# One to four rounds of a threshold search in an iteration of the experts' loop, instead of three in each

## The chip, the cores and the metric

The kernel runs on one core of one Trainium2 chip. Its engines work side by side from their own instruction queues: TensorE (PE, with its weight loads as PEld), VectorE (DVE), ScalarE (ACT), GpSimd (POOL) and SyncE (SP, which here only issues loads). The metric is the device time of one launch in microseconds.

## What is computed

A small language-model tower: an n-gram embedding, an attention block of three branches, and a mixture of 32 experts in which each expert chooses the 256 tokens of 8192 that have the highest probability for it. The change lies in the last part:

```python
k = min(int(bs * C_CAP) // E, bs)             # 8192 // 32 = 256
h = xf @ W_router + b_router
Sm = jax.nn.softmax(h, axis=-1)
G_ek, idx_ek = jax.lax.top_k(Sm.T, k)
tokens = xf[idx_ek]
tok_g = tokens.reshape(NUM_GROUPS, GROUP_SIZE, k, H)
up = jnp.einsum('gjkh,ghf->gjkf', tok_g, W_up) + b_up[:, None, None, :]
act = jax.nn.silu(up).reshape(E, k, D_FF)
Eout = jnp.einsum('ekf,efh->ekh', act, W_down) + b_down[:, None, :]
weighted = G_ek[..., None] * Eout
y = jnp.zeros((bs, H)).at[idx_ek.reshape(-1)].add(weighted.reshape(-1, H))
```

## The kernel before

Embedding, attention and router take the first 950 us of the span. The function `experts` does the rest. It finds for each expert the probability of its 256th token, one bit of the float in a round, over 30 rounds (`BITS`), with a trial value per expert in `cand`. There are two searches, each for 16 experts. The first (h = 0) runs alone ahead of the loop. The second (h = 1) is spread over the first iterations of the loop over the experts, `ROUNDS = 3` rounds in each of the iterations e = 0 to 9; its result is first needed at the end of iteration 9 (`find_over(3)`), for the experts from number 16 on.

A round k is a chain through three engines. VectorE and ScalarE count what lies below the trial value (`count_bit`, L1699 and L1862), TensorE adds the counts over the partitions (`total`, L1491, L1493, L1495), and VectorE settles the bit (`settle_bit`, L1704, L1705, L1708), which writes the next trial value. The last round counts all on VectorE and is added with L1506 and L1507; then the thresholds are turned (L1512).

All engines run programs written out in order by hand. Iteration e of TensorE is `down(e)` (the second product of expert e, L1629), a round's total, `up(e + 1)` (the first product of the next expert, L1614), a round's total, `turn(e + 2)` (transposes of the tokens of the one after, L1599), `unread` (4 products that nobody reads, L1500), and a round's total. These are places 0, 1 and 3 in the new code's count. In iterations 0, 3 and 6 three more experts are ranked (`TRIPLE_AT`): `rank` comes ahead of `up`, `rows_before` (L1579) behind it, and `rows` (L1588) with 8 unread products behind `turn`. Iterations 1 and 10 also place a group of experts (`IN_LOOP`).

VectorE weighs the result of an expert (`weigh`, L1819, into yw) and copies the turned tokens (`copy_x`, L1812); in a ranking iteration it also makes `reached` (L1777) and the slots (`find_rows`, L1787 to L1799). GpSimd issues for each expert two gathers of tokens, four experts ahead (L1968, into xg), and two adding scatters of results (L1977, into out_h); the scatters of expert e wait for yw of e and for the scatters of e - 1 to land. With each gather of a new triple it also waits for the slots of that triple.

Of the kernel before, what the change touches and what calls it, by code (L numbers as in the profile page):

```python
# [43 lines left out]
BITS = 30  # L44
# [1230 lines left out]
def experts(nc, ctx, consts, con, prob, probT, bits, stored, scores, turned, mixed, table, w_up, b_up, w_down, out):  # L1275
# [11 lines left out]
    def sem(name):  # L1287
        return ctx.enter_context(nc.semaphore(name))
# [72 lines left out]
    cand_ok = [sem(f"cand_ok{h}") for h in range(SHARES)]  # L1361
# [34 lines left out]
    def lap(e, buffers):  # L1396

        return (e // buffers + 1) * 16
# [8 lines left out]
    PLACE_BANK = (2, 3, 0, 1, 0)  # L1407
    IN_LOOP = {1: 2, 10: 3, 13: 4}

    ROUNDS = 3  # L1410
    UNREAD_TO = 14

    def rounds_of(e):

        return range(min(e * ROUNDS, BITS), min((e + 1) * ROUNDS, BITS))

    def total_at(h):

# [58 lines left out]
    def _(pe):  # L1477
# [8 lines left out]
        def total(h, k):  # L1486

            pe.wait_ge(cand_ok[h], k + 1)
            if h > 0:
                pe.wait_ge(counted[h], k + 1)  # L1490
            pe.matmul(total_at(h), fours[:], limits[:, 0:1], start=True, stop=False)  # L1491
            pe.wait_ge(counted_a[h], k + 1)
            pe.matmul(total_at(h), less_one[:], count_a[:, h:h + 1], start=False, stop=False)  # L1493
            pe.wait_ge(counted[h], k + 1)
            pe.matmul(total_at(h), less_two[:], count[:, h:h + 1], start=False, stop=True).then_inc(totalled[h], 1)  # L1495
# [19 lines left out]
        def totals(ks):  # L1515
            for k in ks:
                if k < BITS - 1:
                    total(1, k)
                else:
                    total_last(1)  # L1520
                    thresholds(1)
# [70 lines left out]
        def turn(e):  # L1592
            pe.wait_ge(x_in[e % XB], HALVES * lap(e, XB))
            if e >= 2:
                pe.wait_ge(xt_v, e - 1)
            if e - 3 in IN_LOOP:
                pe.wait_ge(chosen_ok, IN_LOOP[e - 3] + 1)
            for half in range(HALVES):
                last = pe.transpose(scores[:, (e % 2) * 512 + half * P:(e % 2) * 512 + (half + 1) * P],  # L1599
                                    xg[:, e % XB, half, 0:C], ident)  # L1600
            last.then_inc(xt_t, 1)
# [55 lines left out]
        turn(1)  # L1657
        for e in range(NE):
            down(e)
            totals(rounds_of(e)[0:1])  # L1660
            if e in TRIPLE_AT:
                rank(TRIPLE_AT[e])
            if e + 1 < NE:
                up(e + 1)
            if e in TRIPLE_AT:
                rows_before(TRIPLE_AT[e])
            totals(rounds_of(e)[1:2])
            if e + 2 < NE:
                turn(e + 2)
            if e in IN_LOOP:  # L1670
                sums(IN_LOOP[e])
            if e in TRIPLE_AT:
                if rounds_of(e):
                    pe.wait_ge(cand_ok[1], rounds_of(e)[1] + 2)
                rows(TRIPLE_AT[e])
            if e in IN_LOOP:
                places_within(IN_LOOP[e])
                places_before(IN_LOOP[e])
            elif e < UNREAD_TO:
                unread(8 if e in TRIPLE_AT else 4, (e + 1) % 2)  # L1680
            totals(rounds_of(e)[2:])

    @block.vector
    def _(dve):
# [30 lines left out]
        def later_count(ks):  # L1715
            for k in ks:
                count_bit(1, k, SPLIT if k < BITS - 1 else HC)

        def later_settle(ks):
            for k in ks:  # L1720
                settle_bit(1, k)
                if k == BITS - 1:
                    keep_thresholds(1)
# [21 lines left out]
        def find_over(g):  # L1745
            compare(over, g, ALU.is_gt).then_inc(over_ok, 1)
# [82 lines left out]
        dve.tensor_scalar(odd[:, 1, :].bitcast(I32), probT[:, HC + SPLIT:2 * HC].bitcast(I32), 1, None, ALU.bitwise_or  # L1829
                          ).then_inc(odd_later, 1)  # L1830
        for e in range(NE):
            first, second, third = (rounds_of(e)[j:j + 1] for j in range(ROUNDS))
            later_count(first)
            weigh(e)
            later_settle(first)
            later_count(second)
            if e in TRIPLE_AT:
                reach(TRIPLE_AT[e])
            later_settle(second)
            if e + 2 < NE:  # L1840
                copy_x(e + 2)
            if e in TRIPLE_AT:
                find_rows(TRIPLE_AT[e])
            later_count(third)
            if e in IN_LOOP:
                choose(IN_LOOP[e])
            later_settle(third)
            if e > 0 and e + 1 in IN_LOOP:
                find_over(IN_LOOP[e + 1])
                find_ties(IN_LOOP[e + 1])  # L1850

    @block.scalar
    def _(act):
        act.activation(less_one[:], K("same"), ACT.Identity, scale=-4.0).then_inc(less_ok, 1)
        act.activation(less_two[:], K("same"), ACT.Identity, scale=-8.0).then_inc(less_ok, 1)
        act.wait_ge(odd_ok, 2)
        act.activation(probT.rearrange("p (h c) -> p h c", h=SHARES)[:, :, (CT - 1) * P:],
                       scores[:, 0:SHARES * P].rearrange("p (h c) -> p h c", h=SHARES), ACT.Identity).then_inc(prob_copied, 1)

        def count_bit(h, k):  # L1860
            act.wait_ge(cand_ok[h], k + 1)
            act.activation(below_a[:], odd[:, h, :], ACT.Sign, bias=cand[:, h:h + 1].bitcast(F32), scale=-1.0,  # L1862
                           accum_out=count_a[:, h:h + 1]).then_inc(counted_a[h], 1)

        def later_count(ks):
            for k in ks:
                if k < BITS - 1:
                    count_bit(1, k)

        with act.Fori(0, BITS - 1) as k:  # L1870
            count_bit(0, k)

        act.wait_ge(bup_in, 16)
        act.activation(warm[:], bup[:, 0:1], ACT.Silu)
        act.wait_ge(far_in, 16)
        act.wait_ge(made_g, 1)

        def keep_sums(g):
            act.wait_ge(sums_t, g + 1)
            at = slice(pairs(g)[0], pairs(g)[-1] + 1)  # L1880
            act.activation(tile_sums[:, :, at], down_bank[:, 0:2 * NE // PAIR].rearrange("t (m j) -> t m j", m=2)[:, :, at],
                           ACT.Identity).then_inc(sums_a, 1)

        def keep_ranks(g):
            e0, e1 = TRIPLES[g][0], TRIPLES[g][-1] + 1
            act.wait_ge(rank_t, g + 1)
            act.activation(ranks[:, e0:e1, 0:P], rank_bank[0:TT, 0:(e1 - e0) * P].rearrange("p (e t) -> p e t", t=P),
                           ACT.Identity).then_inc(rank_a, 1)

        def find_rows(g):  # L1890
            e0, e1, m = TRIPLES[g][0], TRIPLES[g][-1] + 1, len(TRIPLES[g])
            act.wait_ge(row_t, HALVES * g + 2)
            for i, e in enumerate(TRIPLES[g]):
                k = e * HALVES + 1
                act.activation(less[:, k, :], row_bank(1)[:, i * RW:i * RW + P], ACT.Sign,  # L1895
                               bias=K("slotmid")[:, 1:2], scale=-1.0, accum_out=n_less[:, k:k + 1])
            at = slice(e0 * HALVES + 1, (e1 - 1) * HALVES + 2, HALVES)
            act.activation(tile_no[:, at], row_bank(1)[:, 0:m * RW].rearrange("p (i r) -> p i r", r=RW)[:, :, P],
                           ACT.Identity).then_inc(row_a, 1)

        def silu(e):
            act.wait_ge(up_t, e + 1)
            if e >= 2:
                act.wait_ge(down_t, e - 1)
            for c in range(FC):
                n = FP if c < FC - 1 else FP - 1
                k = e // GROUP * FC + c
                last = act.activation(hid[0:n, e % 2, c, :], up_bank[0:n, c * TOPK:(c + 1) * TOPK], ACT.Silu,  # L1908
                                      bias=bup[0:n, k:k + 1])
            last.then_inc(hid_a, 1)  # L1910

        keep_sums(0)
        keep_ranks(0)
        find_rows(0)
        keep_ranks(1)
        keep_sums(1)
        find_rows(1)
        keep_ranks(2)
        find_rows(2)
        act.wait_ge(ones_set, 2)  # L1920
        silu(0)
        act.wait_ge(odd_later, 1)
        for e in range(NE):
            later_count(rounds_of(e)[0:1])
            if e in TRIPLE_AT:
                keep_ranks(TRIPLE_AT[e])
            later_count(rounds_of(e)[1:2])
            if e + 1 < NE:
                silu(e + 1)
            if e in IN_LOOP:  # L1930
                keep_sums(IN_LOOP[e])
            if e in TRIPLE_AT:
                find_rows(TRIPLE_AT[e])
            later_count(rounds_of(e)[2:])

    @block.gpsimd
    def _(pool):
# [103 lines left out]
```

## Time and profile before

| | us |
|---|---|
| median of 3 runs | 1228.16 (1227.95 to 1229.41) |
| profiled execution, its own time | 1231.34 |
| its span, first to last instruction | 1229.6 |
| start of the experts' part (first search) in the span | 950.6 |
| first `down` of the loop | 1013.91 |
| last scatter ends | 1227.4 |

All readings of the timeline are microseconds from the start of the span. "Iteration e" is the stretch from TensorE's `down(e)` to its `down(e + 1)`. "PEclk" and "granted clock" are TensorE's, as a share of 2.4 GHz; it has the two levels 1.00 and 0.50 (1.2 GHz), and a value between them is a mean over a stretch.

### The profile page before, as it was taken

Reading aid. Unit: us, or ns where it says so; the run is one execution under the profiler, and the core shown is the slowest. Engines: PE = TensorE matmul, PEld = TensorE weight load, DVE = VectorE, ACT = ScalarE, POOL = GpSimd, SP = SyncE. Lnnn points to the kernel's source line nnn. Section 1 sums busy time; section 2 is a strip of 40 time slices with the busy share of each in tenths; the row PEclk is TensorE's granted clock in tenths of the full one; section 3 lists DMA queues with packets and bytes.
Section 4 is the critical chain, followed back from the end, with each engine's and each line's share of the span. In section 5 each row is a group of like instructions: output and inputs, shape, how many; then the busy total and the mean of one; then the engine's idle time right before and its main releaser. Section 6 shows DMA issues by size and latency. Waiting matters only on the chain. (4 is left out here: it accounts for less than half of the span.)

```text
span 1229.6 us, 23394 instructions
## 1 busy us (share of the span) xinstructions
PE 1065.2 (87%) x7550; PEld 944.5 (77%) x7550; DVE 830.4 (68%) x2686; ACT 677.6 (55%) x1742; POOL 736.0 (60%) x1200
## 2 busy tenths in 40 slices
PE   5689999999999999999999999999995357788672
PEld 4569888988988898998899899888884135666551
DVE  5346777787877778777777877787676777664220
ACT  0346756756676676666576666666663545434220
POOL 6356676677467547746864775353445027678885
PEclk9989999999999999999999999999997558889876
DMA  3011011010001001010100101000001103344442
GB/s 106 18 33 27 14 29 33 14 36 21 24 25 35 25 10 39 25 30 25 35 26 10 35 25 34 12 10 12 14 16 40 41 18 70 68 81 86 85 71 29
DMA packets 49085, 42.64 MB, mean 35 GB/s; under 512 B 6728, under 2 KB 44488, under 8 KB 48840
## 3 DMA queue, kind: packets, MB, share of 16 engines
q0 software_dynamic: 18432, 22.04, 9.5%
q1 hardware_dynamic: 30536, 19.13, 5.1%
q8 instruction: 62, 1.02, 0.3%
q14 instruction: 55, 0.45, 0.1%
HBM read 27.51 MB, written 13.63 MB: 33 GB/s over the span
## 5 line engine op out<-in xcount | busy, mean ns | idle before, releaser
L657 PE MATMUL mixed<-v,pT 128*128 128x131 f32 x2560 | 318.7, 276 | 3.6 <-DVE o L920 3.2
L657 PEld LDWEIGHTS mixed<-v,pT 128*128 128x128 f32 x2560 | 301.5, 190 | 5.0 <-issue 4.5
L913 DVE TENSOR_REDUCE neg_max<-scores 128x1 f32<-128x1024 f32 (+1 forms) x192 | 198.8, 1035 | 48.9 <-PE scores L444 48.8
L1150 POOL DMA_INDIRECT gram<-in_emb,ids x192 | 189.9, 989 | 64.9 <-issue 52.4
L1078 ACT ACTIVATE probs<-scores,neg_max 128x1024 f32<-128x1024 f32 (+1 forms) x192 | 186.2, 970 | 38.8 <-DVE neg_max L913 38.3
L1087 ACT ACTIVATE pT<-turned 128x512 f32<-128x512 f32 x219 | 130.0, 593 | 74.8 <-PE turned L638 73.9
L1201 POOL TENSOR_TENSOR zb<-row,gate 128x384 f32<-128x384 f32 x64 | 54.5, 851 | 144.2 <-DVE gate L948 143.8
L638 PE MATMUL turned<-con,probs 128*128 128x128 f32 x876 | 126.7, 275 | 7.6 <-ACT probs L1078 3.5
L1977 POOL DMA_INDIRECT out_h<-yw,slots x64 | 102.4, 1601 | 36.1 <-issue 20.6
L638 PEld LDWEIGHTS turned<-con,probs 128*128 128x128 f32 x876 | 101.6, 141 | 22.3 <-ACT probs L1078 8.9
L1968 POOL DMA_INDIRECT xg<-token_table,slots x64 | 64.5, 1008 | 67.6 <-DVE slots L1799 49.0
L919 DVE BATCH_NORM_STATS2 st<-mixed 128x6 f32<-128x128 f32 x192 | 56.1, 292 | 59.3 <-PE mixed L657 57.7
L442 PE MATMUL scores<-k_hi,xT_hi 128*128 128x512 f32 x192 | 82.2, 428 | 0.3 <-DVE k_lo L818 0.3
L956 DVE SCALAR_TENSOR_TENSOR u<-o,gate_r,u 128x128 f32<-128x128 f32 x128 | 78.2, 611 | 4.5
L1087 ACT ACTIVATE pT<-mixed 128x512 f32<-128x512 f32 x101 | 60.0, 594 | 30.5 <-PE mixed L638 30.0
L1908 ACT ACTIVATE hid<-scores,bup 114x256 f32<-114x256 f32 (+1 forms) x96 | 38.4, 471 | 69.3 <-PE scores L1614 69.2
L443 PE MATMUL scores<-k_lo,xT_hi 128*128 128x512 f32 x192 | 75.8, 395 | 0.0
L444 PE MATMUL scores<-k_hi,xT_lo 128*128 128x512 f32 x192 | 75.8, 395 | 0.0
L1629 PE MATMUL mixed<-wd,hid 114*128 114x128 f32 x384 | 61.4, 321 | 9.4 <-issue 9.4
L1218 POOL TENSOR_SCALAR shift<-mv 128x1 f32<-128x1 f32 x64 | 14.6, 229 | 89.4 <-DVE mv L967 87.4
L1205 POOL TENSOR_TENSOR zb<-zb 128x128 f32<-128x128 f32 x128 | 60.6, 474 | 10.0
L1629 PEld LDWEIGHTS mixed<-wd,hid 114*128 114x128 f32 x384 | 55.7, 228 | 12.5 <-issue 12.0
(350 smaller groups left out, 2550.2 us busy)
## 6 DMA issues: line engine op xcount, KB each, us to landing
wd<-in_w_down SPq DMA_DIRECT2D x32, 171.0 KB
token_table<-w SPq DMA_DIRECT2D x16, 320.0 KB, 2.4
out_h<-h SPq DMA_DIRECT2D x16, 256.0 KB, 2.3
gram<-in_emb,ids POOLq DMA_INDIRECT x192, 2.5
wu<-in_w_up SPq DMA_DIRECT2D x8, 170.5 KB, 4.0
w<-in_weights SPq DMA_DIRECT2D x1, 1174.0 KB, 6.4
xg<-token_table,slots POOLq DMA_INDIRECT x64, 3.1
out_h<-yw,slots POOLq DMA_INDIRECT x64
```

Source lines behind the costliest of these rows:

```text
L442: pe.matmul(dst, lhs[0], rhs[0], start=first_one, stop=False)
L443: pe.matmul(dst, lhs[0], rhs[1], start=False, stop=False)
L444: return pe.matmul(dst, lhs[1], rhs[0], start=False, stop=last_one)
L638: last = pe.transpose(dst[:, j * P:(j + 1) * P], probs[:, n % 2, half * 512 + j * P:half * 512 + (j + 1) * P], ident)
L657: last = pe.matmul(mixed[:, 0:C + 3], pT[:, n % 2, j * P:(j + 1) * P], vals[:, 0:C + 3], start=(j == 0), stop=(last_half and j == half * 4 ...
L913: dve.tensor_reduce(neg_max[:, n % 4:n % 4 + 1], scores[:, (n % 2) * S:(n % 2) * S + width], AX_X, ALU.max, negate=True).then_inc(maxed, 1)
L956: last = dve.scalar_tensor_tensor(out=u[:, m, br, :], in0=o[:, n % 4, br, 0:C], scalar=gate_r[:, m, br:br + 1], in1=u[:, m, br - 1, :] if ...
L1078: act.activation(probs[:, n % 2, 0:width], scores[:, (n % 2) * S:(n % 2) * S + width], ACT.Exp, bias=neg_max[:, n % 4:n % 4 + 1], accum_ou ...
L1087: act.activation(pT[:, n % 2, half * 512:half * 512 + 512], shared_bank(TURNED_ON[n, half]), ACT.Identity).then_inc(pT_ok, 1)
L1150: pool.indirect_dma_start(gram[:, t % 4, g, :], None, emb[g], bass.IndirectOffsetOnAxis(ap=ids[:, s, t, g:g + 1], axis=0)).then_inc(gather ...
L1629: last = pe.matmul(down_bank[:, half * C:(half + 1) * C], hid[:, e % 2, c, half * P:(half + 1) * P], wd[:, e % EB, c, :], start=(c == 0), ...
L1977: pool.indirect_dma_start(rows_out, bass.IndirectOffsetOnAxis(ap=slots[:, k:k + 1], axis=0), yw[:, e % EB, half, :], None, compute_op=ALU. ...
```

## The change

The number of rounds in an iteration now comes from a table. The iterations 0 to 9 hold 1, 3, 4, 1, 4, 4, 2, 4, 4 and 3 rounds, where each held 3. The sum is 30 in both. There is a new place 2, directly behind `turn` on TensorE and behind `copy_x` on VectorE. One round sits at place 1; two sit at 1 and 3; three at 0, 1 and 3, as before; four at all places. Everything else keeps its order.

```diff
-    ROUNDS = 3
+    ROUND_AT = (0, 1, 4, 8, 9, 13, 17, 19, 23, 27, BITS)
+    PLACES = 4
     def rounds_of(e):
-        return range(min(e * ROUNDS, BITS), min((e + 1) * ROUNDS, BITS))
+        return range(ROUND_AT[e], ROUND_AT[e + 1]) if e + 1 < len(ROUND_AT) else range(0)
+    def rounds_in(e, place):
+        in_order = ((), (1,), (1, 3), (0, 1, 3), (0, 1, 2, 3))[len(rounds_of(e))]
+        return [k for k, at in zip(rounds_of(e), in_order) if at == place]
...
             down(e)
-            totals(rounds_of(e)[0:1])
+            totals(rounds_in(e, 0))
...
-            totals(rounds_of(e)[1:2])
+            totals(rounds_in(e, 1))
             if e + 2 < NE:
                 turn(e + 2)
+            totals(rounds_in(e, 2))
             if e in IN_LOOP:
                 sums(IN_LOOP[e])
             if e in TRIPLE_AT:
-                if rounds_of(e):
-                    pe.wait_ge(cand_ok[1], rounds_of(e)[1] + 2)
+                for k in rounds_in(e, 1):
+                    pe.wait_ge(cand_ok[1], k + 2)
                 rows(TRIPLE_AT[e])
...
-            totals(rounds_of(e)[2:])
+            totals(rounds_in(e, 3))
...
             later_count(third)
+            later_settle(third)
+            later_count(fourth)
             if e in IN_LOOP:
                 choose(IN_LOOP[e])
-            later_settle(third)
+            later_settle(fourth)
```

ScalarE's list changes in the same way (its counts at places 2 and 3 both stand behind `find_rows`).

TensorE, iteration 4, from the total behind `up(5)` to `down(5)`, before (turned<-... are the three products of a total, scores<-con,xg is `turn`, scores<-slot_bf is `unread`, mixed<-wd,hid is `down`):

```order
L1491 MATMUL turned<-limits,fours 128x1
L1493 MATMUL turned<-count_a,less_one 128x1
L1495 MATMUL turned<-count,less_two 128x1
L1599 MATMUL scores<-con,xg 128x128 x2
L1500 MATMUL scores<-slot_bf,ones_bf 128x256 x4
L1491 MATMUL turned<-limits,fours 128x1
L1493 MATMUL turned<-count_a,less_one 128x1
L1495 MATMUL turned<-count,less_two 128x1
L1629 MATMUL mixed<-wd,hid 128x128 x6
```

and now:

```order
L1497 MATMUL turned<-limits,fours 128x1
L1499 MATMUL turned<-count_a,less_one 128x1
L1501 MATMUL turned<-count,less_two 128x1
L1605 MATMUL scores<-con,xg 128x128 x2
L1497 MATMUL turned<-limits,fours 128x1
L1499 MATMUL turned<-count_a,less_one 128x1
L1501 MATMUL turned<-count,less_two 128x1
L1506 MATMUL scores<-slot_bf,ones_bf 128x256 x4
L1497 MATMUL turned<-limits,fours 128x1
L1499 MATMUL turned<-count_a,less_one 128x1
L1501 MATMUL turned<-count,less_two 128x1
L1635 MATMUL mixed<-wd,hid 128x128 x6
```

A third total stands between `turn` and the unread products, which move behind it.

TensorE, the end of iteration 3 and the begin of iteration 4, before (turned<-ranks,reached is `rows`):

```order
L1588 MATMUL turned<-ranks,reached 128x130 x6
L1500 MATMUL scores<-slot_bf,ones_bf 128x256 x8
L1491 MATMUL turned<-limits,fours 128x1
L1493 MATMUL turned<-count_a,less_one 128x1
L1495 MATMUL turned<-count,less_two 128x1
L1629 MATMUL mixed<-wd,hid 128x128 x6
```

and now:

```order
L1594 MATMUL turned<-ranks,reached 128x130 x6
L1506 MATMUL scores<-slot_bf,ones_bf 128x256 x8
L1635 MATMUL mixed<-wd,hid 128x128 x6
L1497 MATMUL turned<-limits,fours 128x1
L1499 MATMUL turned<-count_a,less_one 128x1
L1501 MATMUL turned<-count,less_two 128x1
```

The total that stood between the unread products and `down(4)` is gone there; iteration 0 reads alike, iteration 6 keeps its total at this place.

## Rows read from the trace of the kernel before

**Rows 1.** The page's second part: the granted clock, in tenths, in 40 slices.

```profile
PEclk9989999999999999999999999999997558889876
```

**Rows 2.** Chain that ended last, in order of time: start, length, what.

```profile
1102.60 0.85 POOL xg L1968
...
1225.84 1.55 POOL out_h L1977
```

**Rows 3.** Timeline, GpSimd: start, length, instruction, [idle before, what ended it].

```profile
1027.78 1.62 POOL L1977 DMA_INDIRECT out_h<-yw,slots  x1 [3.69 <-DVE yw L1819]
...
1051.19 1.62 POOL L1977 DMA_INDIRECT out_h<-yw,slots  x1 [4.11 <-issue]
...
1084.74 1.61 POOL L1977 DMA_INDIRECT out_h<-yw,slots  x1 [0.30 <-issue]
...
1092.23 1.62 POOL L1977 DMA_INDIRECT out_h<-yw,slots  x1 [0.75 <-DVE yw L1819]
```

**Rows 4.** Timeline, TensorE: the starts of `down(0)` to `down(10)`.

```profile
1013.91 1.58 PE L1629 MATMUL mixed<-wd,hid 114*128 114x128 f32 x12 [1.18 <-issue]
...
1023.42 2.91 PE L1629 MATMUL mixed<-wd,hid 114*128 114x128 f32 x12
...
1031.50 1.58 PE L1629 MATMUL mixed<-wd,hid 114*128 114x128 f32 x12
...
1037.25 1.58 PE L1629 MATMUL mixed<-wd,hid 114*128 114x128 f32 x12
...
1046.01 2.77 PE L1629 MATMUL mixed<-wd,hid 114*128 114x128 f32 x12
...
1052.89 1.58 PE L1629 MATMUL mixed<-wd,hid 114*128 114x128 f32 x12
...
1058.67 1.58 PE L1629 MATMUL mixed<-wd,hid 114*128 114x128 f32 x12
...
1067.26 2.91 PE L1629 MATMUL mixed<-wd,hid 114*128 114x128 f32 x12
...
1075.29 1.58 PE L1629 MATMUL mixed<-wd,hid 114*128 114x128 f32 x12
...
1080.98 1.58 PE L1629 MATMUL mixed<-wd,hid 114*128 114x128 f32 x12
...
1087.86 2.93 PE L1629 MATMUL mixed<-wd,hid 114*128 114x128 f32 x12
```

**Rows 5.** Timeline, TensorE, iteration 2: `up(3)`, a total, unread products, a total.

```profile
1033.38 1.53 PE L1614 MATMUL scores<-xT,wu 128*114 128x256 f32 x6
1035.12 0.16 PE L1491 MATMUL turned<-limits,fours 33*128 33x1 f16 x1 [0.21 <-DVE below L1699]
...
1035.53 0.60 PE L1500 MATMUL scores<-slot_bf,ones_bf 128*128 128x256 bf16 x4
1037.04 0.16 PE L1491 MATMUL turned<-limits,fours 33*128 33x1 f16 x1 [0.90 <-DVE below L1699]
```

**Rows 6.** Timeline, TensorE: first total of iteration 0; end of iteration 3.

```profile
1016.36 0.16 PE L1491 MATMUL turned<-limits,fours 33*128 33x1 f16 x1 [0.87 <-DVE below L1699]
...
1043.03 1.05 PE L1500 MATMUL scores<-slot_bf,ones_bf 128*128 128x256 bf16 x8
1045.85 0.16 PE L1491 MATMUL turned<-limits,fours 33*128 33x1 f16 x1 [1.78 <-DVE below L1699]
```

**Rows 7.** Timeline, VectorE, two rounds of the first search, which runs alone.

```profile
966.63 0.22 DVE L1708 SCALAR_TENSOR_TENSOR cand<-turned,if_dropped,if_kept 128x1 f32<-128x1 f32 x1 [0.21 <-PE turned L1495]
...
968.06 0.22 DVE L1708 SCALAR_TENSOR_TENSOR cand<-turned,if_dropped,if_kept 128x1 f32<-128x1 f32 x1 [0.21 <-PE turned L1495]
```

**Rows 8.** Stretches: length, busy PE, PEld, DVE, ACT, POOL, granted clock, DMA share, GB/s.

```profile
1022.40:1029.00 6.60, 5.75 (x24) 4.66 (x24) 3.87 (x16) 1.60 (x5) 2.61 (x3) 0.50 0.23 54
...
1046.30:1049.50 3.20, 3.20 (x17) 2.85 (x17) 1.68 (x7) 0.76 (x2) 0.78 (x1) 0.50 0.23 59
...
1066.80:1073.40 6.60, 6.31 (x28) 4.95 (x29) 3.25 (x16) 1.71 (x5) 4.90 (x4) 0.50 0.48 91
...
1087.20:1093.90 6.70, 6.32 (x31) 5.40 (x31) 3.44 (x8) 0.52 (x2) 5.29 (x4) 0.50 0.36 67
```

**Rows 9.** Stretches, same columns, from the end of `up` on, iterations 2 and 9.

```profile
1034.91:1037.25 2.34, 1.23 (x14) 0.92 (x13) 1.70 (x10) 1.85 (x6) 2.04 (x2) 1.00 0.51 100
...
1084.33:1086.99 2.66, 1.01 (x10) 0.73 (x10) 2.24 (x10) 1.24 (x4) 2.05 (x3) 1.00 0.37 96
```

More of the change, by code:

```diff
@@ L1831, in _ @@
         for e in range(NE):
-            first, second, third = (rounds_of(e)[j:j + 1] for j in range(ROUNDS))
+            first, second, third, fourth = (rounds_in(e, place) for place in range(PLACES))
             later_count(first)
@@ L1923, in _ @@
         for e in range(NE):
-            later_count(rounds_of(e)[0:1])
+            later_count(rounds_in(e, 0))
             if e in TRIPLE_AT:
                 keep_ranks(TRIPLE_AT[e])
-            later_count(rounds_of(e)[1:2])
+            later_count(rounds_in(e, 1))
             if e + 1 < NE:
@@ L1933, in _ @@
                 find_rows(TRIPLE_AT[e])
-            later_count(rounds_of(e)[2:])
+            later_count(rounds_in(e, 2))
+            later_count(rounds_in(e, 3))
     @block.gpsimd
```

## Prediction

> **What bounds the kernel now.** I read the chain that ended last from its end backwards. From 1102.60 to the last instruction at 1225.84 it is GpSimd issuing gathers and scatters [rows 2]. So the end is set by when GpSimd can work through its list, and the question is what it waits for ahead of that. Its timeline answers [rows 3]. Undisturbed, it needs 6.45 us for an expert (two gathers of about 1.0, two scatters of about 1.6, four gaps of 0.3). But it idled 3.69 us ahead of the scatters of expert 1, 4.11 ahead of those of expert 4, and 0.75 ahead of those of expert 10, each time since yw came late; the 4.11 is put down to "issue", but it ends behind the late `down(4)`. From 1092.23 on nothing of this size comes before the last four experts. So the time ends where `down(10)` puts it: yw of expert 10 is what the scatters at 1092.23 wait for, and those start 4.37 us behind `down(10)` at 1087.86 [rows 3, 4]. GpSimd alone would have been ready at 1084.74 + 6.45, plus some tenths for a landing, about 1091.5, so only 0.75 us of slack lies between the two. Every microsecond by which `down(10)` moves later goes to the end whole. By as much as it moves earlier the end gains, as long as GpSimd's own 6.45 us for an expert allow it.
>
> So the sum is over iterations 0 to 9, from 1013.91 to 1087.86, 73.95 us [rows 4]. Their lengths are 9.51, 8.08, 5.75, 8.76, 6.88, 5.78, 8.59, 8.03, 5.69 and 6.88. Two things make them up. **A plain iteration is the chain of its three rounds**: in iteration 2 the totals start at 1035.12 and 1037.04, and TensorE idled 0.21 and 0.90 us for VectorE's counts [rows 5]. **And the granted clock**: the page's slices already show it at 8 and 9 tenths in the slices of the loop, where 9 and more stand through the attention part [rows 1]. Read closer, it is 0.50 in 1022.4 to 1029.0, 1046.3 to 1049.5, 1066.8 to 1073.4 and 1087.2 to 1093.9 [rows 8]. There `down` takes 2.8 to 2.9 us instead of 1.58. Each fall follows a stretch in which TensorE had little to do: behind the unread products of a ranking iteration it stood 1.78 us until VectorE's count was there [rows 6], and ahead of the last round it was busy 1.01 of 2.66 us [rows 9]. What a low clock costs is read by comparing plain iterations: 8.03 (iteration 7, `down` and `up` both slow) against a mean of 5.74 for iterations 2, 5 and 8, so 2.3 us; where only `down` was slow (iteration 4) 6.88, so 1.15. Without these the ten iterations would be 73.95 - 2.3 - 1.15 - 2.3 = 68.2 us.
>
> **The change, part by part, at full clock.**
>
> *The round behind the rows goes, in iterations 0 and 3.* In iteration 3 the unread products end at 1044.08 and `down(4)` starts at 1046.01 [rows 4, 6]. It needs only hid and yw that are long done, so it moves up by 1.93 us: 8.76 becomes 6.8. What is late next is VectorE, which is in `find_rows` until 1044.9, but it weighs expert 4 only when `down(4)` has ended. In iteration 0 the same 1.9 goes, and the first total no longer holds TensorE for 0.87 us [rows 6]: 9.51 becomes 6.6 or so. Iteration 6 keeps its round there and stays at 8.6.
>
> *The round at place 0 goes, in iterations 0, 3 and 6.* But for those 0.87 us it was free: TensorE went down, rank, up, rows_before, and the round ran on the other engines beside it. These three rounds lose their cover.
>
> *Five iterations get a fourth round (2, 4, 5, 7, 8).* Its total, its count on two engines and its settling join a chain that has no slack. The upper bound is the spacing of the last two totals of a plain iteration, 1.92 us, which holds a `copy_x` [rows 5]; the lower one is a round that runs alone, 968.06 - 966.63 = 1.43 [rows 7]. Between places 2 and 3 nothing else stands on VectorE, so I take 1.46: 5.74 becomes 7.2, and yw, copy_x and GpSimd (6.45 us an expert) hide nothing of it, since the chain of rounds is the longest. It waits nowhere anew on GpSimd or SyncE, and no DMA moves.
>
> Iterations 1 and 9 keep their rounds (5.8 and 6.9). The sum at full clock is 6.6 + 5.8 + 7.2 + 6.8 + 7.2 + 7.2 + 8.6 + 7.2 + 7.2 + 6.9 = 70.7 us, against 68.2. **So the edit itself costs 2.5 us; all that can pay for it is the clock.**
>
> **The clock.** Two falls should go: in iterations 0 and 3 TensorE passes from the unread products straight into `down`, worth 2.3 and 1.15. But the five iterations with four rounds become thin. From the end of `up` to the next `down`, iteration 2 had 2.34 us with 1.23 busy, and the clock stayed; iteration 9 had 2.66 with 1.01 busy, and it fell at once [rows 8, 9]. With a fourth round that stretch is 2.34 + 1.46 = 3.8 us with about 1.4 busy: the transposes end, TensorE waits some 1.3 us for the third count, does 0.6 us of unread products, and waits some 0.8 us for the fourth. That is longer and thinner than either. I take it that the clock falls there nearly each time, and that the iteration behind (3, 5, 6, 8, 9) runs slow, with 7 slow as now behind iteration 6. That makes six slow iterations. The bounds are 6 x 1.15 = 6.9 (only `down` slow) and 6 x 2.3 = 13.8 us. Three of the four falls of the trace lasted 6.6 us and one 3.2 [rows 8], so the mean is 2.0 and the term 12.0. The product `down(10)` itself is slow before and after.
>
> The sum: 70.7 + 12.0 = 82.7 us against 73.95, that is +8.75. The profiled execution (1231.34, its span 1229.6) would read 1240.1; the difference is put on the median of the runs: 1228.16 + 8.8 = 1237.0.
>
> One rule is weighed against this. The rows show falls that cost 1.15 and 2.3 us each. The Trainium skill, "TensorE: Matmul & The Clock Gate", Part 1, says that for modelling the ramp penalty is under 1% of a typical kernel's span and should not be fitted to a specific cold count. Going by its advice the clock term would be left as it is, and the time would be 1230.7. The trace agrees with the size, since six times 2.3 is 1.1% of this span, yet the whole difference at stake here is below 1% too.
>
> **The rivals.** A difference below 0.2% (2.5 us) is about what a measurement of this kernel cannot tell from none.
>
> *As many falls as before.* Thin stretches of four rounds are spared, or every second one falls, so that about three slow iterations stay: 70.7 + 5.75 = 76.4 against 73.95, 1230.7. For it: iterations 2, 5 and 8 kept their clock with 0.90 us gaps. Against it: iteration 9.
>
> *The clock falls only behind iteration 6.* The gaps of four rounds are broken up by unread products and totals, each gap under 1.4 us, where the one behind iteration 3's rows had 1.78. Then 70.7 + 2.3 = 73.0 against 73.95, a gain of 0.95: 1227.2.
>
> *The clock does not fall in the loop at all* until the last round. Then 70.7 against 73.95: a gain of 3.25, which GpSimd can take up in full (behind the scatters of expert 0 its own pace reaches expert 10 long before), 1224.9. This is the faster side, decided by whether TensorE's thin stretches stay just dense enough. Against it speaks that iteration 6 still has its 1.78 us of nothing.
>
> *It doesn't reach the end.* GpSimd had idle time that the loop's lateness could fall into. Against it: only 0.75 us of slack at expert 10. Then 1228 to 1229.
>
> **How the numbers follow.** The forecast (five or six slow iterations, +5 to +13) 0.70. As many falls as before 0.12. Only behind iteration 6 0.09. None 0.05. Not at the end 0.04. The lower end takes in the third case at 1227; the upper one is 10.6 (all six at 2.3 us) and two more, for a slow ranking iteration where rank, up and rows all lie on the path, or a third slow product: 1241.5. Slower by over 0.2%: the forecast and over half of the second case, 0.78. Within: 0.16. Faster: 0.06.
>
> **What would show it.** In the timeline of the changed kernel: `down(1)` some 2.9 us earlier, at about 1020.5, and 1.58 us long; iteration 3 with `down(4)` directly behind the unread products; plain iterations of four rounds 7.2 us long at full clock and about 9.5 at the low one; the granted clock at 0.50 behind iterations 2, 4, 5, 7 and 8. The scatters of experts 1 to 4 start earlier than before, those of expert 10 some 9 us later, at about 1101, with GpSimd idle ahead of scatters from expert 7 on. It is wrong if the clock stays at 1.00 through iterations with four rounds; then the time is 1225 to 1231. It is wrong in the round's price if two four-round totals in a row stand closer than 1.43 us or the plain iterations at full clock are not near 7.2.

## The result and the profile after

| | us |
|---|---|
| changed kernel, median of 4 runs | 1235.74 (1232.84 to 1236.22) |
| kernel before, median of 4 runs | 1228.06 (1226.95 to 1229.41) |
| ratio | 1.0055, 95% interval 1.0039 to 1.0072 |
| the profiled execution of after, its own time and span | 1232.84, 1231.0 |

The change makes the kernel slower, by 5 to 9 us. The forecast was 1237.0. The profiled execution of after is the quickest of its four runs, 3 us below the others, which matters below. All lengths are therefore taken from the first `down` on, which started at 1010.5 to 1013.9 in the executions shown here, so that most of what lies ahead of the loop doesn't enter (one thing still does, see x4).

TensorE in after, the starts of `down(0)` to `down(10)` (L1629 before is L1635 now), to be read beside [rows 4]:

```profile
1010.51 1.58 PE L1635 MATMUL mixed<-wd,hid 114*128 114x128 f32 x12 [1.18 <-issue]
...
1016.94 1.50 PE L1635 MATMUL mixed<-wd,hid 114*128 114x128 f32 x12
...
1022.72 1.58 PE L1635 MATMUL mixed<-wd,hid 114*128 114x128 f32 x12
...
1030.03 1.58 PE L1635 MATMUL mixed<-wd,hid 114*128 114x128 f32 x12
...
1036.35 1.50 PE L1635 MATMUL mixed<-wd,hid 114*128 114x128 f32 x12
...
1043.80 1.58 PE L1635 MATMUL mixed<-wd,hid 114*128 114x128 f32 x12
...
1051.18 2.23 PE L1635 MATMUL mixed<-wd,hid 114*128 114x128 f32 x12
...
1061.13 2.00 PE L1635 MATMUL mixed<-wd,hid 114*128 114x128 f32 x12
...
1069.57 2.91 PE L1635 MATMUL mixed<-wd,hid 114*128 114x128 f32 x12
...
1079.23 2.91 PE L1635 MATMUL mixed<-wd,hid 114*128 114x128 f32 x12
...
1088.54 2.12 PE L1635 MATMUL mixed<-wd,hid 114*128 114x128 f32 x12
```

The ten iterations last 6.43, 5.78, 7.31, 6.32, 7.45, 7.38, 9.95, 8.44, 9.66 and 9.31 us, 78.03 in all, against 73.95. Iterations 0 and 3 shrank by 3.1 and 2.4 us. The four-round iterations at full clock (2, 4, 5) take 7.3 to 7.5. From iteration 6 on the clock is low again and again. The stretches of after, with the columns of [rows 8] (the granted clock is the third number from the right), first three thin stretches from the end of `up` to the next `down` (iterations 2, 4 and 5), then four stretches at the low clock, which follow iterations 5, 6, 7 and 8:

```profile
1026.23:1030.03 3.80, 1.48 (x15) 0.94 (x16) 2.78 (x13) 2.62 (x7) 1.12 (x2) 1.00 0.39 92
1039.90:1043.80 3.90, 1.61 (x15) 1.02 (x16) 2.81 (x13) 2.61 (x7) 2.87 (x4) 1.00 0.50 98
1047.01:1051.18 4.17, 1.55 (x16) 1.01 (x16) 3.09 (x15) 2.71 (x9) 3.53 (x3) 1.00 0.43 89
1052.00:1055.30 3.30, 3.30 (x16) 2.68 (x16) 1.34 (x4) 1.07 (x3) 2.69 (x3) 0.50 0.47 67
1062.20:1065.50 3.30, 3.30 (x14) 2.50 (x12) 2.18 (x11) 0.96 (x4) 0.92 (x1) 0.50 0.34 88
1069.10:1075.70 6.60, 6.30 (x28) 4.94 (x29) 3.26 (x16) 1.80 (x6) 2.90 (x3) 0.50 0.23 58
1079.30:1086.00 6.70, 6.70 (x30) 5.20 (x29) 3.22 (x14) 2.35 (x7) 2.86 (x3) 0.50 0.23 54
```

Three thin stretches of nearly the same content (1.48, 1.61 and 1.55 us busy of 3.8 to 4.2) ended differently. Behind the first two the next `down` took 1.58 and 1.50 us, behind the third it took 2.23, and the clock was 0.50 from 1052.0 on.

GpSimd in after, the first scatter of experts 7, 8, 9 and 10, beside [rows 3]:

```profile
1064.58 1.61 POOL L1987 DMA_INDIRECT out_h<-yw,slots  x1 [2.50 <-DVE yw L1826]
...
1073.92 1.62 POOL L1987 DMA_INDIRECT out_h<-yw,slots  x1 [3.24 <-DVE yw L1826]
...
1083.59 1.61 POOL L1987 DMA_INDIRECT out_h<-yw,slots  x1 [3.54 <-DVE yw L1826]
...
1092.64 1.62 POOL L1987 DMA_INDIRECT out_h<-yw,slots  x1 [2.95 <-DVE yw L1826]
```

GpSimd now idles 2.5 to 3.5 us ahead of each of these four. The scatters of expert 10 start 82.13 us behind `down(0)`, against 1092.23 - 1013.91 = 78.32 before. The span from `down(0)` to the last instruction grew from 215.7 to 220.5 us. That is +4.8 in this execution: its span is 1.4 us longer than the one of before, and its loop started 3.4 us earlier.

### The profile page after: what moved, and what is told of

Same layout as the page of the kernel before. It is cut to its first block and busy times, and to the rows that moved or that the text cites. A ratio compares the mean times of both kernels' runs of the same rounds, so it can differ in the third digit from the quotient of the medians.

```text
span 1231.0 us, 23392 instructions
## 1 busy us (share of the span) xinstructions
PE 1062.0 (86%) x7548; PEld 941.2 (76%) x7550; DVE 829.5 (67%) x2686; ACT 677.7 (55%) x1742; POOL 735.7 (60%) x1200
## 5 line engine op out<-in xcount | busy, mean ns | idle before, releaser
L1635 PE MATMUL mixed<-wd,hid 114*128 114x128 f32 x384 | 60.4, 318 | 6.5 <-issue 6.5
L638 PE MATMUL mixed<-con,probs 128*128 128x128 f32 x404 | 61.5, 275 | 3.0 <-ACT probs L1078 2.0
```

Source lines behind the costliest of these rows:

```text
L638: last = pe.transpose(dst[:, j * P:(j + 1) * P], probs[:, n % 2, half * 512 + j * P:half * 512 + (j + 1) * P], ident)
L1635: last = pe.matmul(down_bank[:, half * C:(half + 1) * C], hid[:, e % 2, c, half * P:(half + 1) * P], wd[:, e % EB, c, :], start=(c == 0), ...
```

## The experiments

Theory 1 is the forecast's: at full clock the change costs some 2.5 us, since rounds leave places where other work covers them, and the clock adds the rest. Its rivals are that the rounds alone cost what is seen and the clock is a symptom (2), that a round costs the same wherever it stands (3), and that GpSimd can take up lateness. The kernels of one group ran on one chip with the same runs of the kernel before: x1 to x4 against a median of 1229.36, x5 to x8 against 1228.42.

**x1, the changed kernel again.** No edit.

> The changed kernel once more, unchanged, for a second profiled execution of it. In the first one the ten iterations took 78.0 us, and the granted clock stayed at 1.00 through iterations 2 and 4 (four rounds each) and fell only behind 5, 6, 7, 8 and 9. Theory 1 (the forecast's clock term): where the thin stretches of four rounds fall decides, so another execution shows the clock at 0.50 behind other iterations too, 2 or 4 among them, and ten iterations of 80 to 84 us, as the median of the runs, 3 us above the profiled one, asks for. Rival (the clock behind 2 and 4 never falls; the runs differ by something else): the same five falls and again 78 us, whatever the time. Time against the kernel before: +5 to +9 us in both.

Measured: 1234.93 us, ratio 1.0041 (1.0023 to 1.0058). This profiled execution took 1237.41 us, span 1235.6, and its ten iterations 80.44 us. Its low stretches:

```profile
1031.70:1038.40 6.70, 6.10 (x27) 5.11 (x27) 2.15 (x9) 1.53 (x5) 4.20 (x4) 0.50 0.37 77
1048.80:1055.50 6.70, 6.61 (x29) 5.10 (x29) 3.22 (x15) 2.02 (x6) 4.25 (x5) 0.50 0.32 63
1059.00:1062.30 3.30, 3.30 (x18) 2.95 (x17) 0.85 (x4) 0.00 (x0) 0.52 (x1) 0.50 0.15 40
1069.30:1072.50 3.20, 3.20 (x15) 2.74 (x15) 1.92 (x8) 0.90 (x3) 0.00 (x0) 0.50 0.11 28
1082.90:1089.60 6.70, 6.24 (x29) 4.96 (x27) 4.15 (x17) 2.29 (x6) 3.55 (x4) 0.50 0.28 51
```

The same program now has its clock low behind iterations 2 and 4, which it kept in the first execution, and kept it behind 7. So an iteration with four rounds doesn't lose the clock each time. Which ones do differs between executions, and with it the length of the loop (80.44 against 78.03). Theory 1 holds, the rival of this run falls.

**x2, the changed kernel with TensorE's waits filled.**

```diff
+            if rounds_in(e, 2):
+                unread(10, (e + 1) % 2)
             totals(rounds_in(e, 2))
...
-                unread(8 if e in TRIPLE_AT else 4, (e + 1) % 2)
+                if e in TRIPLE_AT:
+                    unread(22 if rounds_in(e, 3) else 8, (e + 1) % 2)
+                elif BITS - 1 in rounds_of(e):
+                    unread(14, (e + 1) % 2)
+                else:
+                    unread(10 if rounds_in(e, 3) else 4, (e + 1) % 2)
```

> The changed kernel with the waits of TensorE filled: ten unread products ahead of and ten behind the total at place 2, 22 behind the rows of iteration 6, 14 ahead of the last round, where none, 4, 8 and 4 stood. No round moves, and the fillers are shorter than the waits they fill (1.34 and 0.87, 1.7, 1.3 us). Theory 1 (the edit costs about 2.5 us, the rest of its loss is the clock): the clock stays at 1.00 from iteration 0 to 10, iterations of four rounds take 7.3 us, the ten iterations 71 to 72 us, against 73.95 in the kernel before, and the product of expert 10 is 1.3 us quicker too: 1224 to 1226, 2 to 4.5 us below the kernel before and 10 to 12 below the changed one. Rival 2 (the rounds themselves are what the change loses; the clock is a symptom): the time stays within 2 us of the changed kernel, 1234 to 1237.

Measured: 1226.82 us (1222.86 to 1230.5), ratio to before 0.9974 (0.9960 to 0.9987). TensorE in iteration 2, from the third round's total on:

```profile
1027.33 1.25 PE L1506 MATMUL scores<-slot_bf,ones_bf 128*128 128x256 bf16 x10
1028.83 0.16 PE L1497 MATMUL turned<-limits,fours 33*128 33x1 f16 x1 [0.25 <-DVE below L1713]
...
1028.99 1.25 PE L1506 MATMUL scores<-slot_bf,ones_bf 128*128 128x256 bf16 x10
1030.46 0.16 PE L1497 MATMUL turned<-limits,fours 33*128 33x1 f16 x1 [0.22 <-DVE below L1713]
```

And the whole loop in one stretch, `down(0)` to `down(10)`:

```profile
1011.04:1081.40 70.36, 61.40 (x495) 47.46 (x495) 53.25 (x227) 37.47 (x113) 53.18 (x41) 1.00 0.43 74
```

The fillers (117 to 125 ns each, 2.58 us for 22 and 1.25 for ten) fit into the waits, the clock is 1.00 throughout, and the loop takes 70.36 us. That is 7.7 and 10.1 us less than in the two executions of the changed kernel, with more work on TensorE and every round where it was. Rival 2 falls: the clock is a cause. The median fell 8.1 us below that of x1, less than the 10 to 12 expected, and 1226.82 lies above the expected 1224 to 1226. The trace shows one reason. The expectation counted 1.3 us for a quicker `down(10)`, but what the scatters of expert 10 wait for is VectorE's weighing (L1819, here L1833). Ahead of it VectorE compares the probabilities with the new thresholds (L1742 and the two instructions behind it), and this takes nearly as long as the slow `down(10)`, which ends at 1090.79. VectorE in before, then in x2:

```profile
1088.17 1.01 DVE L1742 TENSOR_TENSOR over<-prob,thr 128x512 bf16<-128x512 f32 x1
...
1090.82 0.61 DVE L1819 TENSOR_SCALAR yw<-mixed,xg 128x128 f32<-128x128 f32 x2 [0.20 <-PE mixed L1629]
```

```profile
1081.72 1.02 DVE L1756 TENSOR_TENSOR over<-prob,thr 128x512 bf16<-128x512 f32 x1
...
1084.11 0.60 DVE L1833 TENSOR_SCALAR yw<-mixed,xg 128x128 f32<-128x128 f32 x2
```

In before VectorE waited only 0.20 us for the slow `down(10)`. In x2 it doesn't wait at all, and the scatters start 4.12 us behind `down(10)` instead of 4.37: a gain of 0.25 us, not 1.3.

**x3, three rounds everywhere, waits filled.** The filling of x2, and the table that restores the placement of before:

```diff
-    ROUND_AT = (0, 1, 4, 8, 9, 13, 17, 19, 23, 27, BITS)
+    ROUND_AT = (0, 3, 6, 9, 12, 15, 18, 21, 24, 27, BITS)
```

> Three rounds in each iteration as in the kernel before, with TensorE's waits filled in the same way: 22 unread products behind the rows of iterations 0, 3 and 6, ten in plain iterations, 14 ahead of the last round. Theory 1: the three falls in the loop go (2.3, 1.15 and 2.3 us) and the slow product of expert 10 (1.3): ten iterations of 68.2 us, 1221 to 1222, 6 to 7 us below the kernel before. Against the filled changed kernel it is 2.5 to 3.5 us quicker, which is the cost of the edit at full clock. Rival 2 (the clock is a symptom): within 1 us of the kernel before.

Measured: 1223.78 us, ratio 0.9954 (0.9939 to 0.9969). The loop:

```profile
1011.02:1078.90 67.88, 58.80 (x473) 45.98 (x474) 53.63 (x227) 37.25 (x113) 50.87 (x40) 1.00 0.43 76
```

67.88 against 68.2 worked out. The median is above the expected 1221 to 1222. Here GpSimd's own list sets the end: the scatters of expert 10 start 5.79 us behind `down(10)` at 1078.90, where 4.12 were enough in x2, and wait for the scatters ahead of them to land:

```profile
1084.69 1.62 POOL L1994 DMA_INDIRECT out_h<-yw,slots  x1 [0.44 <-DMA out_h<-yw,slots]
```

**x2 less x3 is the change at full clock: 70.36 - 67.88 = 2.48 us in the loop, 3.0 in the medians.** And the clock alone had cost the kernel before 73.95 - 67.88 = 6.1 us.

**x4, another table with the cover kept, waits filled.**

```diff
-    ROUND_AT = (0, 1, 4, 8, 9, 13, 17, 19, 23, 27, BITS)
+    ROUND_AT = (0, 2, 5, 9, 11, 15, 18, 20, 24, 27, BITS)
...
-        in_order = ((), (1,), (1, 3), (0, 1, 3), (0, 1, 2, 3))[len(rounds_of(e))]
+        in_order = ((), (1,), (0, 1), (0, 1, 3), (0, 1, 2, 3))[len(rounds_of(e))]
```

> Another table: 2, 3, 4, 2, 4, 3, 2, 4, 3 and 3 rounds, and the two rounds of a ranking iteration stand at places 0 and 1, ahead of the rows, where other work runs beside them; the waits are filled as in the other two. Theory 1 says that what the change lost at full clock is the cover of the rounds at place 0 of ranking iterations: with it kept and only the round behind the rows moved, iterations take 7.5, 5.8, 7.3, 6.8, 7.3, 5.8, 6.8, 7.3, 5.8 and 6.9, sum 67.3 us, one below the filled kernel before; with GpSimd's own 6.45 us for an expert close behind, 1219.5 to 1221.5. Rival 3 (a round costs the same wherever it stands): the sum is that of the filled kernel before, 68.2, or above it, 1222 to 1225.

Measured: 1222.68 us (1221.39 to 1225.81), ratio 0.9947 (0.9928 to 0.9966), the quickest of all kernels here, though its interval overlaps with x3's and the median is above the expected 1219.5 to 1221.5. The loop:

```profile
1011.71:1077.76 66.05, 57.39 (x461) 44.53 (x461) 52.33 (x224) 37.63 (x113) 51.10 (x40) 1.00 0.44 78
```

66.05 us, 1.8 below x3; the expectation was 67.3. But about half of the 1.8 us comes from where the loop is counted from. The first total of iteration 0, in x3 and then in x4:

```profile
1013.47 0.16 PE L1497 MATMUL turned<-limits,fours 33*128 33x1 f16 x1 [0.87 <-DVE below L1713]
```

```profile
1013.22 0.17 PE L1497 MATMUL turned<-limits,fours 33*128 33x1 f16 x1
```

In x3 VectorE begins this count 1.48 us behind `down(0)`, at 1012.50, and TensorE waits 0.87 us for it. In x4, where the clock was low until 1010.0, `down(0)` came late against VectorE: the count begins 0.21 us behind it, at 1011.92, and is ready in time. It isn't the table that removes this wait: in x7 below, which has the placement of before, the clock was low until 1010.0 too, the first total starts at 1013.27 without a wait, and iteration 0 takes 8.58 us instead of 9.51. So at the same start x4 would be some 1.0 us below x3, an estimate from 1.83 - 0.87, and the medians are 1.1 us apart.

The lengths of iterations give the price of each place at full clock, from the starts of `down` in x2, x3 and x4:

| | rounds at | x | length, us |
|---|---|---|---|
| iteration 6 | 0, 1, 3 | x3 | 8.59 |
| iteration 6 | 1, 3 | x2 | 8.36 |
| iteration 6 | 0, 1 | x4 | 6.72 |
| iteration 3 | 0, 1, 3 | x3 | 8.70 |
| iteration 3 | 0, 1 | x4 | 6.56 |
| iteration 3 | 1 | x2 | 6.32 |
| iteration 7 | 0, 1, 3 | x3 | 5.69 |
| iteration 7 | 0, 1, 2, 3 | x2 | 7.33 |

In a ranking iteration the round at place 0 costs 0.24 us, the one behind the rows 1.9 to 2.1. A fourth round in a plain iteration costs 1.64. Rival 3 falls. Iteration 0 is left out of the table, since its round at place 0 costs 0.22 us where `down(0)` came late (6.55 in x4, 6.33 in x8) and by x3's wait 0.87 more where it did not.

**x5, the table of x4 without the filling** (`unread` as in the changed kernel).

> The table of the covered kernel (2, 3, 4, 2, 4, 3, 2, 4, 3, 3 rounds; in ranking iterations at places 0 and 1) without the filling products. At full clock its ten iterations took 66.05 us. Theory 1: the clock falls behind some of the iterations with four rounds (2, 4, 7) and behind the last round, each fall 1.15 to 2.3 us, two or three falls: 69 to 72 us in the loop, 1224 to 1227, between the filled one (1222.7) and the kernel before (1229.4). Rival (with the cover kept the clock no longer matters): 1222 to 1223.

Measured: 1226.85 us (1221.28 to 1231.43), ratio 0.9984 (0.9967 to 1.0002): between x4 and the kernel before, as theory 1 has it, with a wide scatter of runs; the interval reaches 1.0002, so that it is quicker than before is not shown. The loop took 71.09 us; the clock was low twice, behind iterations 2 and 4, and stayed up through iteration 7 with its four rounds:

```profile
1030.50:1037.20 6.70, 6.05 (x29) 5.20 (x30) 3.47 (x14) 2.34 (x7) 4.21 (x4) 0.50 0.38 80
1047.60:1054.30 6.70, 6.15 (x26) 4.79 (x27) 3.51 (x16) 1.90 (x7) 4.32 (x4) 0.50 0.32 63
1054.40:1082.70 28.30, 20.51 (x160) 15.52 (x158) 22.10 (x93) 16.00 (x47) 21.87 (x17) 1.00 0.46 76
```

Two falls cost 71.09 - 66.05 = 5.0 us, 2.5 each.

**x6, the changed kernel, thinner.**

```diff
-                unread(8 if e in TRIPLE_AT else 4, (e + 1) % 2)
+                unread(8 if e in TRIPLE_AT else 0 if rounds_in(e, 2) else 4, (e + 1) % 2)
```

> The changed kernel without the four unread products of the iterations with four rounds, so that TensorE's stretch from up to the next down holds only totals and transposes. Theory 1: the clock falls behind each of the iterations 2, 4, 5, 7 and 8, and behind 6 and 9 as before: at least five slow iterations, the loop 82 to 85 us against 78.0 and 80.4 in the two executions of the changed kernel, 1236 to 1240. Rival (the falls of the changed kernel come from elsewhere, the unread products don't matter): the same 1235.

Measured: 1237.99 us, ratio 1.0073 (1.0049 to 1.0098). The loop took 83.10 us, with the clock at 0.79 on average:

```profile
1011.33:1094.43 83.10, 61.91 (x371) 47.29 (x371) 52.30 (x225) 37.98 (x113) 52.56 (x41) 0.79 0.36 63
```

Less work on TensorE (20 products fewer) made the loop 2.7 and 5.1 us longer than in the two executions of the changed kernel. The times alone don't separate it from the changed kernel: the intervals of the ratios overlap with that of x1. But the one trace of it has the expected fall behind each of the five iterations with four rounds (these five stretches follow iterations 2, 4, 5, 7 and 8), and one more behind 6, from 1067.8 to 1071.2:

```profile
1030.30:1037.00 6.70, 6.21 (x27) 5.12 (x27) 2.04 (x9) 1.42 (x5) 4.14 (x4) 0.50 0.39 81
1047.30:1054.00 6.70, 6.62 (x29) 5.11 (x29) 3.21 (x15) 2.03 (x6) 4.24 (x5) 0.50 0.32 63
1057.60:1060.80 3.20, 3.20 (x18) 2.85 (x17) 0.83 (x4) 0.00 (x0) 0.41 (x1) 0.50 0.15 37
...
1074.60:1081.30 6.70, 5.82 (x24) 4.66 (x24) 3.83 (x16) 2.20 (x6) 3.33 (x4) 0.50 0.31 60
1084.90:1091.60 6.70, 6.58 (x29) 5.22 (x30) 3.21 (x15) 1.99 (x6) 2.73 (x3) 0.50 0.20 52
```

So iterations 3, 5, 6, 7, 8 and 9 were slow, six of ten, and they cost 83.10 - 70.36 = 12.7 us, 2.1 each. That is the state that the forecast had put down for the changed kernel itself.

**x7, the product of expert 10 delayed in the kernel before.**

```diff
         for e in range(NE):
+            if e == 10:
+                unread(20, 1)
             down(e)
```

> The kernel before with 20 unread products right ahead of down(10), nothing else changed. They take 2.2 us at full clock and 4.3 at the low one, so down(10) starts 2.2 to 4.3 us later. Theory 1 says that only 0.75 us of slack lie between that product and the end: the time rises by 2 to 4 us, by the shift of down(10) less at most 0.75 us. Rival (GpSimd's idle time takes up the lateness): no change beyond 0.5 us.

Measured: 1231.99 us, ratio 1.0025 (1.0008 to 1.0041), 3.6 us above the median of before, 3.1 by the ratio. TensorE:

```profile
1085.36 3.88 PE L1500 MATMUL scores<-slot_bf,ones_bf 128*128 128x256 bf16 x20
1089.07 1.50 PE L1629 MATMUL mixed<-wd,hid 114*128 114x128 f32 x12
```

The fillers took 3.88 us, mostly at the low clock. The clock was at 1.00 again from 1088.6 on, so that `down(10)` itself took 1.50 instead of 2.93; whether the fillers brought it back, one trace can't show. The scatters of expert 10 start 80.27 us behind `down(0)` instead of 78.32. Part of the shift is hidden by the shorter iteration 0 (see x4), so it is better counted from `down(9)`:

```profile
1092.03 1.62 POOL L1979 DMA_INDIRECT out_h<-yw,slots  x1 [3.05 <-DVE yw L1821]
```

From `down(9)` to these scatters it is 1092.03 - 1078.49 = 13.54 us against 1092.23 - 1080.98 = 11.25 before, 2.3 more; from `down(9)` to the last instruction 151.0 against 148.6, 2.4 more. The medians moved by 3.6, within an interval of 1 to 5 us. GpSimd doesn't take the lateness up.

**x8, x4 with one round moved** from place 0 of iteration 0 to a fourth place in iteration 5. The edit is shown against x4.

```diff
-    ROUND_AT = (0, 2, 5, 9, 11, 15, 18, 20, 24, 27, BITS)
+    ROUND_AT = (0, 1, 4, 8, 10, 14, 18, 20, 24, 27, BITS)
```

> The filled covered kernel with one round moved: iteration 0 has one round instead of two (none at place 0), iteration 5 four instead of three. Theory 1 (a round at place 0 of a ranking iteration is nearly free, 0.24 us there; a fourth round costs 1.6): iteration 0 takes 6.3 instead of 6.55 us, iteration 5 7.3 instead of 5.7, and the loop 67.4 instead of 66.05; the end follows by at most that, 0.3 to 1.4 us, since GpSimd's own list is close. Rival 3 (a round costs the same wherever it stands): the loop stays at 66 us.

Measured: 1223.52 us, ratio 0.9962 (0.9947 to 0.9976). The loop took 1079.47 - 1011.96 = 67.51 us against 66.05, +1.46 (+1.35 expected); iteration 0 took 6.33 instead of 6.55, iteration 5 took 7.32 instead of 5.70. The medians of the two kernels differ by 0.8 us in the same direction and their ratios by 1.8; the intervals overlap, so the end's shift is not shown by the times. In both executions the clock was low ahead of a late `down(0)`.

## Why the prediction was right, and where its size was off

*What sets the end.* Right for a loop that gets longer: lateness ahead of the scatters of expert 10 reaches the end (x7), and in after GpSimd waits for yw ahead of experts 7 to 10. The link is looser than the forecast had it in three ways. What yw of expert 10 waits for is VectorE's comparing with the new thresholds, which the last round releases together with `down(10)`, and the product's own length hardly counts (0.20 us in before, nothing in x2). In the other direction GpSimd's list soon becomes the limit (x3). And from the first scatter of expert 10 to the last scatter of all it takes 1225.84 - 1092.23 = 133.6 us in before, 134.6 in after and 135.2 in x2, which moves the end by up to 1.6 us without the loop.

*The two stretches that shrink.* Nearly right: 3.1 and 2.4 us in after, with the clock kept (forecast 2.9 and 2.0). The round behind the rows was worth 2.1 us in iteration 3, not 1.9, and the one at place 0 was not free but cost 0.24.

*The price of a fourth round.* Mis-sized a little: 1.46 forecast, 1.64 measured. The forecast had priced it by the round that runs alone. In the loop the spacing of the last two totals is 1029.88 - 1028.25 = 1.63:

```profile
1028.25 0.16 PE L1497 MATMUL turned<-limits,fours 33*128 33x1 f16 x1 [1.34 <-DVE below L1706]
...
1029.88 0.16 PE L1497 MATMUL turned<-limits,fours 33*128 33x1 f16 x1 [0.87 <-DVE below L1706]
```

The errors cancel: the five iterations with four rounds took 0.1 us each more than forecast, and iterations 0, 3 and 6 took 6.31, 6.32 and 8.36 us in x2 where 6.6, 6.8 and 8.6 were forecast. The sum at full clock was put at 70.7 and 68.2, and x2 and x3 show 70.36 and 67.88. **The edit at full clock costs 2.48 us, forecast 2.5**; that it fits so closely is partly luck.

*The clock.* The mechanism was right, and the term too large. The forecast had six slow iterations of 2.0 us in after, 12.0 us. The two executions show 78.03 - 70.36 = 7.7 and 80.44 - 70.36 = 10.1 us. The step that failed is "the clock falls there nearly each time". Of the five thin stretches it fell behind three in the first execution (5, 7 and 8) and behind four in the second (2, 4, 5 and 8). With the fall behind 6 that makes four and five slow iterations instead of six, at 1.9 and 2.0 us each; the 2.0 us were right, the count was not. Where the stretch held even less (x6) it fell behind all five, in the one execution that was traced. The side of before was well sized: 5.75 forecast, 6.1 by x3. Together the change costs 2.5 us by the edit and 1.6 to 4.0 by more time at the low clock, 4.1 to 6.5 in the loop. The medians moved by 5.0 (ratio of x1) to 7.7 us, where 8.8 was forecast.

What stays open is why one thin stretch loses the clock and the next, with nearly the same content, doesn't. The runs show only that it differs between executions of one program.

*The rivals.* "Only behind iteration 6" and "not at all" fall with the traces, "it doesn't reach the end" with x7; "as many falls as before" was nearer than its 12% says: it put the loop at 76.4 us and the forecast at 82.7, and the two executions show 78.03 and 80.44. For modelling, the Trainium skill ("TensorE: Matmul & The Clock Gate", Part 1) puts the ramp penalty below 1% of a typical span and advises against fitting it to a specific count of cold products. The forecast read this as leaving the clock term as it was, which gave 1230.7. It also called its own 1.1% of the span an agreement, though that is above 1%; measured, the term is 7.7 to 10.1 us, 0.6 to 0.8% of the span, so here the size agrees. But x2 and x3 show that it is larger than the edit's whole cost of 2.5 us, and what the change adds to it (1.6 to 4.0) is as large as that cost.

## What to carry to other kernels

Work on a serial chain is free only where something else covers it: before moving a step out of a crowded iteration, ask which of its places were covered there and take away the uncovered one (here the round behind the rows, 1.9 to 2.1 us in iterations 3 and 6) and not the covered one (0.24 us there). Where an engine's clock depends on what it does, a move that thins out its stretches can lose more than the move itself, and products that nobody reads, sized to fit into a wait, are cheap against that. On the path they are not: in x7 20 of them cost 2.3 us net. Both together (x4) gave 0.9947 of the kernel before; most of it is the filling, which alone (x3) gave 0.9954, and the difference is within the intervals.

A length counted from one instruction of one engine isn't free of what lies ahead: with `down(0)` late against VectorE, the same iteration 0 took 8.58 us instead of 9.51.

## What the runs showed of the hardware

TensorE's clock fell to 0.50 behind iteration 5 of after although no wait in that stretch was longer than 1.34 us: it fell behind 4.17 us with 1.55 us busy, in several pieces, and it stayed at 1.00 behind 3.90 us with 1.61 busy. So one long gap was not needed for a fall here. The same program had its low stretches in different iterations in two executions, whose times were 1232.84 and 1237.41 us; 2.4 us of this difference lie in the loop, so some of what looks like scatter of the time is this. With the waits filled, the clock held at 1.00 for 66 to 70 us in four kernels (x2, x3, x4 and x8), in x2 with TensorE busy for 61.40 of 70.36 us; in x5, without them, it held at 1.00 for 28.30 us with TensorE busy for 20.51.
